# Edge-filter stage of a graph network kernel: two accumulation tables in DRAM in place of four

## The reference, cut to what matters

```python
# N_NODES = 6250, E = 106250, features 128; h is the layer-normalised, rectified x
def _L1_gnn_ref(x, f_ij, rcut_ij, idx_i, idx_j, W_in2f, W_f1, b_f1, W_f2, b_f2, W_o1, b_o1, W_o2, b_o2):
    h = x @ W_in2f.T
    Wij = smu(f_ij @ W_f1.T + b_f1) @ W_f2.T + b_f2
    Wij = Wij * rcut_ij[:, None]
    x_ij = h[idx_j] * Wij
    agg = segment_sum(x_ij, idx_i, num_segments=h.shape[0])
    return smu(agg @ W_o1.T + b_o1) @ W_o2.T + b_o2

x = x + _L0_gnn_ref(relu(layernorm(x)), ...)                              # batch norm, graph convolution
x = x + _L1_gnn_ref(relu(layernorm(x)), edge_attr_20, edge_weight, src, dst, ...)
x = x + _L2_gnn_ref(relu(layernorm(x)), src, dst, ...)                    # four edge convolutions, segment max
x = x + _L3_gnn_ref(relu(layernorm(x)), edge_index, ...)                  # two graph convolutions
```

## Time and profile before

| | us |
|---|---|
| median of 3 executions | 11393.48 |
| lowest and highest of them | 11347.6 and 11399.97 |
| the profiled execution, own time | 11520.23 |
| the profiled execution, span of the core | 11518.5 |

### The profile page before, as it was taken

How to read it: one execution, slowest core, us unless ns; L and a number is a source line. 1 busy time by engine, 2 the same in 40 slices (tenths; PEclk the granted TensorE clock), 3 DMA queues, 4 the chain that set the end, 5 groups by cost and what they waited for, 6 DMA issues and landing times. The chain is left out here.

```text
span 11518.5 us, 121592 instructions
## 1 busy us (share of the span) xinstructions
PE 8143.9 (71%) x34932; PEld 4146.4 (36%) x35457; DVE 5554.7 (48%) x11902; ACT 820.8 (7%) x2270; POOL 6674.3 (58%) x6440
## 2 busy tenths in 40 slices
PE   4777748888757776677757777477774777667774
PEld 2333237777733332333332333233322333233331
DVE  4455434444445554444545554455544554445554
ACT  2000021111130000100000000100001000010000
POOL 4555568888835555555555555555555555555555
PEclk8888867777778888888878888788887888878887
DMA  4333435555532222222222222222223222322223
GB/s 166 124 129 128 139 88 77 77 77 76 67 106 84 85 85 86 78 80 84 84 81 82 81 85 82 74 85 85 85 84 95 84 85 83 94 79 84 84 83 104
DMA packets 580217, 1042.14 MB, mean 90 GB/s; under 512 B 149064, under 2 KB 419250, under 8 KB 525900
## 3 DMA queue, kind: packets, MB, share of 16 engines
q0 software_dynamic: 298368, 418.22, 17.3%
q1 hardware_dynamic: 278650, 620.49, 15.5%
q10 hardware_dynamic: 2940, 1.00, 0.0%
HBM read 492.11 MB, written 555.62 MB: 91 GB/s over the span
## 5 line engine op out<-in xcount | busy, mean ns | idle before, releaser
L997 POOL DMA_INDIRECT WORK<-table,stage x5124 | 4904.5, 957 | 4178.1 <-DVE WORK L1102 2412.7
L1145 PE MATMUL bank<-TF,XF 128*128 128x512 bf16 x16800 | 5594.1, 414 | 2073.2 <-issue 1029.5
L1080 DVE TENSOR_TENSOR TF<-AF,bank 128x3584 bf16<-128x3584 bf16 x1225 | 2472.3, 2018 | 3645.1 <-remote 2758.8
L1145 PE MATMUL bank<-TF,Z 128*128 128x512 bf16 x8400 | 3467.4, 413 | 181.0 <-issue 176.0
L1145 PEld LDWEIGHTS bank<-TF,XF 128*128 128x128 bf16 x17150 | 1742.5, 104 | 4604.4 <-issue 1902.5
L1312 POOL DMA_INDIRECT acc<-TOT,stage x832 | 1298.0, 1560 | 272.0 <-issue 196.4
L1145 PEld LDWEIGHTS bank<-TF,Z 128*128 128x128 bf16 x8575 | 902.2, 105 | 1410.2 <-issue 577.4
L1102 DVE SCALAR_TENSOR_TENSOR WORK<-WORK,RESET 128x128 f32<-128x128 f32 x2928 | 1028.0, 351 | 352.3 <-DVE WORK L1102 21.3
L1102 DVE SCALAR_TENSOR_TENSOR WORK<-WORK,KEEP 128x128 f32<-128x128 f32 x2196 | 771.2, 351 | 266.0 <-DMA WORK<-table,stage 24.8
L1021 ACT COPY TOT<-bank 128x512 f32<-128x512 f32 x175 | 102.4, 585 | 8486.9 <-PE bank L1145 4343.7
L1517 DVE SCALAR_TENSOR_TENSOR BASE<-bank,WEIGHT,BASE 128x128 f32<-128x128 f32 x832 | 234.1, 344 | 756.4 <-PE bank L1387 721.5
(11 more groups left out here) (249 smaller groups left out, 3089.4 us busy)
## 6 DMA issues: line engine op xcount, KB each, us to landing
run_rows<-WORK SPq DMA_DIRECT2D x357, 1024.0 KB
WORK<-table,stage POOLq DMA_INDIRECT x5124
fill_rows<-BASE SPq DMA_DIRECT2D x52, 1024.0 KB
WORK<-fill_rows SPq DMA_DIRECT2D x104, 512.0 KB
AF<-src_keys SPq DMA_DIRECT2D x175, 128.0 KB
table<-TF SPq DMA_DIRECT2D x56, 384.0 KB
acc<-TOT,stage POOLq DMA_INDIRECT x832
acc<-Z SPq DMA_DIRECT2D x12, 1024.0 KB
```

Source lines behind the costliest of these rows:

```text
L997: pool.indirect_dma_start(RUN[:, b, k, :], None, table, table_row(table, stage[:, b, k:k + 1]))\
L1080: dve.tensor_tensor(OHOT[:, (h * CHUNKS + c) % 2, :, :].rearrange("p k (a e) -> p k a e", e=SPREAD), EKEYS[:, 1 - h, :].rearrange("p (a e) ...
L1145: i = nc.tensor.matmul(bank(2 + h)[:, 0:BATCH], PIECES[n][:, c * PART + k, :], OHOT[:, ((h + 1) * CHUNKS + c) % 2, k, :], start=c + k + n ...
```

## The change

ACCS goes from 4 to 2. The adds of the edge-filter stage go to two tables in turn, so before step j POOL waits for the landing of the add of step j - 2, not j - 4. The source block of TOT is chosen by the step in the quad as before. ACT's wait counts two adds of a quad on each of two semaphores. The update loads two tables per group and sums them with one instruction. The head clears two tables, since its loop runs over ACCS.

```diff
-ACCS = 4
+ACCS = 2
...
                         pool.indirect_dma_start(
                             acc_dram[a],
                             bass.IndirectOffsetOnAxis(stage[:, h, j % HALF:j % HALF + 1].bitcast(u32), 0),
-                            TOT[:, j // QUAD % 2, a * F:(a + 1) * F], None, compute_op=ALU.add).then_inc(added[a], 16)
+                            TOT[:, j // QUAD % 2, j % QUAD * F:(j % QUAD + 1) * F], None, compute_op=ALU.add).then_inc(added[a], 16)
...
                     for a in range(ACCS):
-                        wait(act, added[a], (n - 1) * 16)
+                        wait(act, added[a], (n - 1) * (16 * QUAD // ACCS))
...
                     dve.wait_ge(acc_in[g % 2], 16 * ACCS * (g // 2 + 1))
-                    st.did(dve.tensor_tensor(acc[0], acc[0], acc[1], ALU.add))
-                    st.did(dve.tensor_tensor(acc[2], acc[2], acc[3], ALU.add))
-                    st.join()
-                    dve.tensor_tensor(acc[0], acc[0], acc[2], ALU.add).then_inc(rows_used, 1)
+                    dve.tensor_tensor(acc[0], acc[0], acc[1], ALU.add).then_inc(rows_used, 1)
```

## The result

| | before | changed |
|---|---|---|
| median, us | 11396.72 (4 executions) | 11706.19 (4 executions) |
| lowest and highest, us | 11347.6, 11461.04 | 11688.23, 11751.48 |
| profiled execution, us | 11520.23 | 11704.78 |

The ratio is 1.0266, with a 95% interval of 1.0233 to 1.0300: slower by 309 us, where 268 were forecast, and inside the range. The two profiled executions differ by only 184.5 us of span. The seven passing stages, which the change does not touch, took 8796 us in the one of before against 8712 in that of the change, 84 us the other way; the updates and stretches between them took another 24 us less. So the change is read from its own stages.

A forecast was written before the change was run, and what follows sets the result against it. POOL's pace of issuing adds was taken to bound the edge-filter stage. Adds +285, head clearing -11 and update -6 gave +268 us on 11393.5, so 11661 us, with a range of 11500 to 11750.

The forecast's parts named there:

- What bounds the stage: Edge-filter stage: POOL's pace, one add every 1.864 us, sets it; PE, DVE and ACT have room.
- Landing time from ACT's copies: Edge-filter adds: an add lands 3.3 us after its start at the median, 3.53 on the mean.
- The wake-up: POOL's start after a landed add it waited for: 0.77 us in a loop, 0.21 with a constant wait.
- the lower bound: Adds on POOL: with only 0.21 us from landing to POOL's start, they cost +125 us.
- The upper bound: Adds on POOL: a second wait and increment cost 0.5 us in every fourth step, +350 us in all.
- The sum for the adds: Adds on POOL: waiting two steps back makes POOL wait in most pairs of steps, +285 us.
- The Trainium skill's figure: Adds on POOL: 2.15 us per 64 KB DMA, counted from the end of the issue, would give +311 us.
- The clearing: Head: half of the table clearing, 6.55 MB, goes and a stall ends sooner, -11 us.
- The update: Update after the adds: fewer loads and sums before the first groups, later groups unchanged at 10.32 us, -6 us.
- Rival 1: Adds on POOL: POOL starts 0.21 us after a landing and only late landings cost; +108 us, 11501 us, chance 0.15.
- rival 2: Adds on POOL: landings grow or the second wait counts at full price; +350 - 17, 11727 us, chance 0.15.
- rival 3: Adds on POOL: landings are short enough that no wait remains, only the gains are left; 11376 us, chance 0.05.

The follow-up runs named there:

- written-out loop: The changed kernel (two tables) with POOL's loop over the adds written out, so waits have a constant and no counter increment behind them: 11612.76 us, ratio 1.0092.
- both edits of the head: The kernel before with table clearing moved from the head to the first passing stage and x saved and restored in partition order: ratio 0.9980.

## Why the prediction was right, and where not

*What bounds the stage.* Right. POOL's pace of 1.864 us per add set it before, landing plus wake-up set it after, and PE, DVE and ACT had the room that the waits of the earlier trace rows promised.

*Landing time from ACT's copies*. 3.3 us at the median and 3.53 on the mean were inferred with 0.2 us for ACT's wake-up. The landing time shown on the quick chip is 3.3 us at the median, and the changed kernel's records give 3.31 and 3.45. The 0.2 us was near: on the quick chip ACT's copy starts 0.18 us after the landing in the unchanged kernel, but 0.07 in the changed one, so ACT's pairs did not stay at 3.5 us as forecast but fell to 3.41.

*The wake-up*. This decided it. 0.77 us was taken from two other places in the trace where POOL waits in a loop, 0.21 as the bound from a constant wait; the adds show 0.77 and 0.27. The written-out loop shows what the lower bound would have been, +109 us for the predicted +125. The upper bound charged a second hold 0.5 us in every fourth step; it costs 0.15 (0.92 in place of 0.77).

*The sum for the adds.* +285 was predicted, +299 measured on the first chip and +273.5 on the last. The mean alone, +237, would have been too low, as argued; the tail is worth 87 us on one chip, and 116 from one chip to another.

*The Trainium skill's figure* ("DMA: Bandwidth & Descriptors", section "Anatomy of one DMA — SWDGE (gpsimd) path"), about 2.0 us plus the bytes over 436 GB/s, gave an estimate of +311 for the adds when it was counted from the end of the issue. The measured landing is 3.3 - 1.56 = 1.7 us behind the issue's end, less than its 2.15, and the tail, which the figure leaves out, made up for it on the first chip.

*The clearing.* Wrong. "The engines seem starved by the full DMA" was the step that failed: -11 us was predicted, -0.5 and -1.3 measured. Two things that happened together were taken for cause and effect. With the traffic gone from the stretch the stall stayed, and on another chip the traffic stayed and the stall was gone. What causes the stall is open.

*The update.* -6 predicted, -5.2 and -7.8 measured. The steady 10.3 us per group behind ACT held.

*Sum.* 268 predicted, 309 measured, of which the stages account for 293. Of the 25 us between 293 and the forecast, 14 are the adds, 10 the head and 1 the update. The other 16 are within the interval. That two parts missed in opposite directions on the last chip, adds 11 us under and the head 10 over, is luck for its total of 264. Rival 1 (a short wake-up) is the written-out kernel; of rival 2 neither longer landings nor a second hold at full price was seen; rival 3 (no wait) fell.

## What to carry to other kernels

Where an engine waits for its own DMA some steps back, compare distance times pace with landing plus wake-up, and take the tail with it: here 3.73 us against 4.07 cost 270 to 300 us, and waiting one add further back (5.59 us) cost 5. The wake-up after a real wait does not show in a trace in which nothing waits; look for another place where the engine does, in the same form: here a wait with a register value and an increment behind it cost half a microsecond more than a constant one. And a stall beside a full DMA is not yet a stall because of it: take the traffic away before it is put into a sum.

## What the runs showed of the hardware beyond that

The same program took about 11400 to 11500 us on some chips and 9070 us on two others, and most of the difference lies in the passing stages: around 1250 us each on the first kind and 919 to 926 on the second, while the adds took 1549 us on both. On the first kind DVE waits there for releases that no record explains. The waits of DVE between 3400 and 4500 us, in the first trace of before (us in total, times, longest):

```profile
DVE TF L1080 <- remote: 346.2, 56, 11.8
DVE TF L1080 <- PE bank L1145: 73.9, 19, 8.1
```

and in the unchanged kernel on the quick chip, where DVE waits for POOL's gathers instead:

```profile
DVE WORK L1102 <- DMA WORK<-table,stage: 227.7, 196, 4.4
DVE TF L1080 <- PE bank L1145: 17.2, 20, 1.4
```

In the head, on the first kind, the trace shows what such a release is: in the changed kernel's trace PE's last transpose ends at 86.6 us, the record of its semaphore update stands at 108.1, and ACT starts at 108.11. The update is 21.5 us late, among others that mostly stand 0.7 us or a multiple of it apart, until some 3 us after POOL's last gather ends at 112.2. In the trace with both edits of the head the records between 90 and 105 us are as sparse, 7 or 8 in 5 us, though the DMA share is 0.07. What makes one chip deliver updates late and another not, no run here tells. On both kinds two tables lose 264 to 309 us: the adds' landings (3.31 and 3.28 us at the median) and POOL's start 0.77 us after them read the same on both.
